# A two-layer kernel on one core: another order for tile 4, the transposes of tiles 1 and 5, and the bias rows of the feed-forward

## What is computed

```python
x = x + matmul(fake_quant(layernorm(x)), fake_quant(ctx_4096))      # ctx_4096 (2, 2048, 2048)
y = layernorm(x)
base_out = matmul(y, kernel) + bias                                  # kernel (2048, 2048), bias (2048,)
A_eff = einsum('bn,nri->bri', gate, lora_A)                          # y as 8 groups of 256 rows
B_eff = einsum('bn,nor->bor', gate, lora_B)
delta = B_eff (A_eff y) + lora_B_shared (lora_A_shared y)            # rank 32 each
out = x + base_out + delta
```

## Time and profile before

| | us |
|---|---|
| median of the runs | 1049.54 |
| profiled execution | 1046.42 |
| its span | 1044.9 |
| PE busy in it | 991.1 (95%), 4663 matmuls |
| DVE busy | 536.2 (51%) |
| ACT busy | 297.0 (28%) |
| POOL busy | 209.8 (20%) |
| share of PE in the chain that ended last | 71% |

### The profile page before, as it was taken

One profiled execution on the slowest core, in us unless ns is written; L12 is line 12 of the kernel. 1 busy time (PEld: TensorE's weight loads), 2 busy tenths in 40 slices (PEclk: granted clock), 3 DMA queues, 4 the chain that ended last, 5 costly groups with the idle time before them and its releaser, 6 DMA issues.

```text
span 1044.9 us, 12005 instructions
## 1 busy us (share of the span) xinstructions
PE 991.1 (95%) x4663; PEld 460.3 (44%) x4663; DVE 536.2 (51%) x756; ACT 297.0 (28%) x213; POOL 209.8 (20%) x233
## 2 busy tenths in 40 slices
PE   2898999898999999999999999998999999999996
PEld 1343444353544444444444444444554444444442
DVE  7766858968554565553423765877542032014010
ACT  4663422253131142232214521363230021012000
POOL 3001100021113013212411643320104004004010
PEclk9999999999999999999999999999999999999999
DMA  8699982859655346446699851767824024014010
GB/s 364 240 307 380 355 306 39 186 115 216 172 183 198 123 152 200 158 149 206 233 294 284 323 204 71 160 123 151 211 107 156 31 101 161 20 40 150 10 50 20
DMA packets 139863, 181.43 MB, mean 174 GB/s; under 512 B 112688, under 2 KB 112688, under 8 KB 127280
## 3 DMA queue, kind: packets, MB, share of 16 engines
q1 hardware_dynamic: 125040, 117.99, 39.1%
q0 software_dynamic: 13632, 58.73, 15.5%
q10 hardware_dynamic: 1152, 4.19, 1.0%
HBM read 124.26 MB, written 29.36 MB: 147 GB/s over the span
## 4 chain that ended last, share of the span: by engine, by line
PE 71%; DVE 10%; DMA 6%; ACT 5%; issue 4%; SPq 1%; POOL 1%; POOLq 0%; ACTq 0%; DVEq 0%
PE psum L1005 17%; PE psum L1187 16%; PE psum L1188 16%; PE psum L1189 16%; PE psum L1210 2%; DVE ring L1446 2%; DMA stage<-in_ctx_in 1%; PE psum L1067 1%; DVE hl L1492 1%; ACT ring L785 1%; DMA bias_sb<-in_bias 1%; DMA xn<-in_x 1%; DMA stage<-in_w 1%; PE psum L1199 1%; PE psum L1198 1%
## 5 line engine op out<-in xcount | busy, mean ns | idle before, releaser
L1187 PE MATMUL psum<-ring,lhs 128*128 128x512 f16 x1016 | 385.8, 380 | 12.6 <-issue 8.5
L1188 PE MATMUL psum<-ring,lhs 128*128 128x512 f16 x1016 | 385.8, 380 | 0.0
L1189 PE MATMUL psum<-ring,lhs 128*128 128x512 f16 x1016 | 385.6, 380 | 0.0
L1005 PE MATMUL psum<-ring,lhs 128*128 128x512 bf16 x1024 | 227.8, 381 | 3.6 <-DVE ring L1412 2.1
L1187 PEld LDWEIGHTS psum<-ring,lhs 128*128 128x128 f16 x1016 | 99.5, 98 | 135.2 <-issue 11.0
L1005 PEld LDWEIGHTS psum<-ring,lhs 128*128 128x128 bf16 x1024 | 100.3, 98 | 126.0 <-issue 4.2
L1189 PEld LDWEIGHTS psum<-ring,lhs 128*128 128x128 f16 x1016 | 99.6, 98 | 120.3 <-issue 0.8
L1188 PEld LDWEIGHTS psum<-ring,lhs 128*128 128x128 f16 x1016 | 99.5, 98 | 118.5 <-issue 0.5
L1499 DVE SCALAR_TENSOR_TENSOR x<-psum,sc,x 128x512 f32<-128x512 f32 (+1 forms) x64 | 45.2, 746 | 191.2 <-PE psum L1199 190.4
L649 POOL TENSOR_TENSOR x<-x,bias_sb 128x512 f32<-128x512 f32 (+1 forms) x64 | 86.6, 1377 | 190.9 <-ACT x L916 130.4
L785 ACT ACTIVATE ring<-stage,sc 128x2048 f16<-128x2048 f32 x32 | 63.6, 1999 | 170.1 <-PE psum L1189 137.8
(11 more groups left out here) (168 smaller groups left out, 656.5 us busy)
## 6 DMA issues: line engine op xcount, KB each, us to landing
stage<-in_w SPq DMA_DIRECT2D x38, 1024.0 KB, 6.3
stage<-in_ctx_in SPq DMA_DIRECT2D x30, 1024.0 KB, 8.1
out<-x POOLq DMA_DIRECT2D x64, 256.0 KB, 3.2
x<-in_x POOLq DMA_DIRECT2D x8, 1024.0 KB, 11.9
xn<-in_x POOLq DMA_DIRECT2D x8, 1024.0 KB, 6.8
x<-in_x POOLq DMA_DIRECT2D x4, 2048.0 KB, 14.7
lhs<-in_lora_a POOLq DMA_DIRECT2D x4, 1024.0 KB, 12.0
lhs<-in_lora_b SPq DMA_DIRECT2D x4, 1024.0 KB, 9.7
```

The source lines that it names most:

```text
L1005: last = pe.matmul(psum[:, t, :], lhs_q[:, k, t * P:(t + 1) * P], ring_q[:, g, j % 2, u, :], start=(k == 0), stop=(k == KT - 1 and not by_pe))
L1187: pe.matmul(psum[:, t, :], hi, ring[:, g, 0, u, :], start=(kk == 0), stop=False)
L1188: pe.matmul(psum[:, t, :], hi, ring[:, g, 1, u, :], start=False, stop=False)
L1189: last = pe.matmul(psum[:, t, :], lo, ring[:, g, 0, u, :], start=False, stop=False)
```

## The change

- SP: in block 0 both halves of tile 1 are transposed right behind tile 0, ahead of the load of weight group 2; before, the high half stood ahead of it and the low half behind it. Tile 5's transposes stand ahead of `load_a` 2.
- ACT: group 2 of block 0 is converted ahead of the root of tile 2. The split, the next root and the row term of tile 4 stand ahead of `product_p` 0 and `b_groups`.
- DVE: `product_p` 0 and the two `b_pair` stand behind tile 4 instead of behind tile 3.
- PE: in the pair, group 2's products with the top half of the weights (`top_group`) wait only for ACT's conversion; the products with the rest (`rest_group`) follow once DVE is done. The same matmuls in all.
- POOL: the bias row of block 0 is fetched by `first_bias` at the place of before; the rows of blocks 1 to 3 by `next_bias`, right after the sums of the block before (in batch 0's block 0 after the reduction of the maxima), so ahead of that block's stores and of the next loads of x.

```diff
@@ w_block @@
                         turn_y(b, 0)
-                        turn_high(b, 1)
-                    if g == 2 and isinstance(j, int) and j == 0:
-                        turn_low(b, 1)
+                        turn_y(b, 1)
@@ SP, block 0 @@
                 if b == 0:
                     w_peaks_block(1)
+                turn_y(b, 5)
                 load_a(b, 2)
-                turn_y(b, 5)
@@ POOL @@
             def add_bias(b, j, bb, reg):
+                pool.wait_ge(bias_in, (bb + 1) * 16)
                 if reg:
-                    pool.wait_ge(biased, bb * TILES)
                     pool.sem_inc(go, 1)
-                else:
-                    if b:
-                        pool.wait_ge(with_col, NBLK * TILES)
-                    pool.wait_ge(psum_full, (blk(b, 0, NBLK - 1) + 1) * TILES)
-                pool.dma_start(bias_sb[:, :], bias_row[:, bass.ds(j * NW, NW)].to_broadcast([P, NW])).then_inc(bias_in, 16)
-                pool.wait_ge(bias_in, (bb + 1) * 16)
                 for t in range(TILES):
...
+            def first_bias(b):
+                if b:
+                    pool.wait_ge(with_col, NBLK * TILES)
+                pool.wait_ge(psum_full, (blk(b, 0, NBLK - 1) + 1) * TILES)
+                pool.dma_start(bias_sb[:, :], bias_row[:, 0:NW].to_broadcast([P, NW])).then_inc(bias_in, 16)
+
+            def next_bias(j, bb):
+                pool.wait_ge(biased, (bb + 1) * TILES)
+                pool.sem_inc(go, 1)
+                pool.dma_start(bias_sb[:, :], bias_row[:, bass.ds(j * NW + NW, NW)].to_broadcast([P, NW])).then_inc(bias_in, 16)
...
+                first_bias(b)
                 add_bias(b, 0, blk2(b, 0), False)
                 if b == 0:
                     largest(4, MX_W, PW_W)
+                next_bias(0, blk2(b, 0))
                 store(b, 0, blk(b, 1, 0))
...
                     add_bias(b, j, j + blk2(b, 0), True)
+                    next_bias(j, j + blk2(b, 0))
                     if b + 1 < NBATCH:
                         for i in range(1, LNB):
@@ ACT, block 0 @@
                 split_hi(b, 1)
+                w_groups(b, 0, [2])
                 root(b, 1, 2)
-                w_groups(b, 0, [2, 3])
+                w_groups(b, 0, [3])
                 split_hi(b, 2)
...
                 norm2_rows(3)
+                norm2_rows(4)
                 product_p(b, 0)
                 b_groups(b, 0)
-                for t in (4, 5, 6):
-                    norm2_rows(t)
+                norm2_rows(5)
+                norm2_rows(6)
                 product_p(b, 1)
@@ PE @@
+            def top_group(t, g):
+                for u in range(GU):
+                    for h in range(2):
+                        y = lhs[:, h, g * GU + u, t * P:(t + 1) * P]
+                        pe.matmul(psum[:, t, :], y, ring[:, g, 0, u, :], start=False, stop=False)
+
+            def rest_group(t, g):
+                for u in range(GU):
+                    hi = lhs[:, 0, g * GU + u, t * P:(t + 1) * P]
+                    pe.matmul(psum[:, t, :], hi, ring[:, g, 1, u, :], start=False, stop=False)
...
-                    for g in range(2, NG):
-                        pe.wait_ge(converted, grp_w(b, 0, g) + 1)
-                        for t in range(2):
-                            base_group(t, g)
+                    pe.wait_ge(act_conv, act_w(b, 0, 2) + 1)
+                    for t in range(2):
+                        top_group(t, 2)
+                    pe.wait_ge(converted, grp_w(b, 0, 2) + 1)
+                    for t in range(2):
+                        rest_group(t, 2)
+                    pe.wait_ge(converted, grp_w(b, 0, 3) + 1)
+                    for t in range(2):
+                        base_group(t, 3)
@@ DVE, block 0 @@
                 for t in range(3, TILES):
-                    if t == 4:
+                    if t == 5:
                         product_p(b, 0)
                         for h in range(2):
                             b_pair(b, 0, h)
```

## The result

| | before | after |
|---|---|---|
| median of the runs, us | 1050.85 | 1044.13 (1041.86 to 1044.75) |
| ratio | | 0.9941, 95% interval 0.9925 to 0.9956 |
| profiled execution, us | 1046.42 | 1044.01 |
| its span, us | 1044.9 | 1042.4 |

The change takes 6 to 7 us off the median where 12.5 were forecast, and the time is 7 us above the forecast of 1037.0, just outside the range. Before and after stand within 2% of each other, as forecast. Note that the two profiled executions differ by only 2.4 us; the first experiment shows why. One timed execution of before, of 4784.78 us, and one of a later kernel, of 1621.07 us at a mean granted clock of 0.618, lie far outside the rest and enter no ratio.

The account below looks back on a forecast made before the run. PE's waits (15.8 us) and slow clock (1.7) bound what can be won. 0 - 0.2 + 2.15 + 3.44 + 2.96 + 1.7 - 0.3 + 2.7 = 12.5 us off the 1049.54 median gives 1037.0, range 1033 to 1043.

Parts of the forecast that it names:

- What bounds the kernel: PE, busy 95%; from 160 us only its 15.8 us of waits and 1.7 us of slow clock can be won.
- Tile 1: Transposes ahead of group 2's load: PE's 2.7 us given back later, 0 in batch 0, loss of 0.2 in batch 1.
- rival 3: Late group 2 delays tile 3, both batches; 8.4 us load costs 4 to 4.5; loss chance 0.07, slower than before 0.03.
- Tile 4: Done ahead of LoRA on VectorE, its transposes land before PE asks: waits of 2.15 and 3.44 us go.
- Tile 5: Transposes ahead of slab load_a(2) in batch 0: PE's 2.96 us gap goes, and 1.7 of slow clock behind it.
- rival 2: SP's queue in batch 0 spoils tile 5 (1 us) or last slab (2), slow stretch returns (1.7): 1041.4; chance 0.15.
- The last slab: load_a(3) in batch 0: PE arrives earlier than VectorE's chain gains, 0.3 us of new waiting, bounds 0 and 2.
- The bias row: Early fetch in batch 0's loop: second x load 6.7 us earlier, block 2's 2.7 us of waits gone, 4 spare.
- rival 1: Bias row is no cause: the load of x at 339.74 goes no earlier; 1039.7 us, chance 0.1.
- The range: 1033 to 1043 us around 1037.0, with group 2's landing and median drift below, three rivals above.
- The rule on the clock: An idle gap between PE's matmul bursts drops its clock; 1.7 us counted at tile 5, though a 3.44 gap showed none.

Follow-up runs that it names:

- the first experiment: The kernel before, run again with no edit: median 1050.85 us, profiled span 1050.6 us against 1044.9 in the profile the forecast used.
- the one-element operation: The changed kernel plus a one-element tensor_tensor on GpSimd behind each partition_all_reduce, to load its code back early: 1041.65 us, 0.9924 of before.

## Why the forecast was 7 us too low, point by point

Two terms of the sum failed: tile 1 (-0.2, and it cost 3) and the bias row (2.7, and it brought 0). The two terms of tiles 4 and 5 came, but not each from its own edit.

- **What bounds the kernel** was right: the gains and losses of all kernels are PE's waits and slow stretches. But the base was one execution with one slow stretch, and the second profile of the same kernel has five such lengths (17 us). The step "The median of the runs is 1049.54, 3.1 above it; off that it is 1037.0" carried the 3.1 us over as if no edit could touch them, though part of them is slow stretches. Of the 8.2 us between the spans of the second execution of before and of the change (1050.6 and 1042.4), 2.7 are waits (15.7 and 13.0) and some 6 are clock (7.6 us lost in slow stretches against 1.6).
- **Tile 1: "gives 0 in batch 0 ... a loss of 0.2" in batch 1.** It cost 3. In batch 0 the steps held in kind: load issued at 190.05 (189.3 forecast), ScalarE at 196.09 (195.5), short waits at groups 2 and 3, tile 3 0.5 late. The low half landed at 193.6, not 191.7, as 4.4 us is the landing of an undisturbed transpose and this one took 6.9. The step that failed is batch 1, where I wrote "the orders are the same and the waits smaller" and did not read the queue. There the load had gone out in time in which SyncE had nothing else to issue (668.54, the low half at 670.74); behind it, it lost not the length of an issue but the whole wait for y_lo(1), and then met three other transfers. This is near rival 3 in its mild form, 4 to 4.5 us for a load of 8.4 us: it took 5.9 in batch 0 and 8.9 in batch 1. I gave it 0.07. The landing time alone was not what I had to fear: the later issue cost more.
- **Tile 4: 2.15 + 3.44.** Right, step by step: high half at 227.16 (226.6 forecast), low half at 229.38 (228.6), landed at 234.0 (233.5), no wait in either batch. Its size was too small, because it also does what I put down to tile 5.
- **Tile 5: 2.96 + 1.7.** The gap and the stretch are gone, with the low half landing at 245.6 (245 forecast), but not by this edit. The step "load_a(2) ... held SP to 247.6 (7.78 us)" took the slab for the cause; the cause was the two weight loads in flight ahead of it. My rival 2 had it right ("whenever a transpose follows a 1 MB load"), and the term did not use it. Tile 4's part moves those 7 us earlier and the hold falls to 2.55. The edit is worth 1 to 2 us at a place that I had not looked at.
- **The last slab: -0.3.** It landed in time in batch 0. The wait that came instead is 0.66 us at 261.35 for VectorE's evict2: PE gained more than VectorE's chain, as I had written, but the first thing that PE needs from that chain is a free bank of PSUM and not the slab.
- **The bias row: 2.7.** 0. "The configuration starts at about 309.8: adds from 317.0" took 7.2 us for the reload, 12.7 were needed; with the slower adds that took 3.3 us of the 6.7. And "4 to spare" took the landing time of x as fixed at 5.7 us, when its issue moved right onto two weight loads, to 10.0. The outcome is that of rival 1 (1039.7, chance 0.1), for a reason that it did not name: x did go earlier. The laps even lost some: PE comes to blocks 2 and 3 earlier by what it won at tiles 4 and 5, and the chain that begins with x does not. There is a gap of 2.93 us where there were 1.24 and 1.47, with a slow stretch behind it, and one of 1.47 where there was none.
- **The range.** Rivals 1 and 3 came true together: 12.5 - 2.7 - 3.0 - 0.7 at evict2 is 6.1 us, what was measured. That it fits so well is in part luck, as it leaves out the 4.0 us that the laps lost and the clock's gain beyond 1.7. I had priced each rival by itself. The 1033 to 1043 took in each of the two and not both.
- **The rule on the clock** (the Trainium skill, TensorE: Matmul & The Clock Gate, "Why this matters for your kernels"): an idle gap between bursts drops the clock. The traces agree for 23 gaps of 31. The 3.44 us of the first profile, not followed by a slow stretch, had made me doubt it; the same gap in the second profile, 3.47 us, was.

Not settled: the parts don't add up exactly. 11.4 us for tile 4's part, 1 to 2 for tile 5's, 0 for the row and -3 for tile 1's make 9 to 10, and the change has 6.2; the change without tile 1's part has 9.1 with an interval of 3 us to both sides. Whether tile 4's part loses 2 us in company, or the intervals hide it, these runs don't tell. As half of its gain is clock, and a gap elsewhere can bring a slow stretch back, the parts need not add up. Nor was anything tried against the 2.6 us at tile 1's low half.

## What to carry to other kernels

When a step is moved past another on a queue that issues in order, ask what that queue did in the time between: a load that went out while the queue had nothing else is not late by an issue but by the whole wait of the step put ahead of it, and this has to be read in each batch by itself. A long issue of a transpose belongs to what is in flight ahead of it as much as to the transpose, so moving the transfers ahead of it may cure it alone. And a transfer that is issued earlier lands earlier only if it doesn't run into others there: when a chain starts from one load, let the loads that nobody waits for yet go behind it (4.5 us here for two waits).

## What the runs showed of the hardware

- **The clock.** The same program, much the same gaps: from 160 us on 3.4 us at 0.50 in one execution, 17 us in another. Of the gaps of 2.15 to 3.95 us 23 of 31 were followed by such a stretch; 3.44 and 3.45 us once each were not.
- **GpSimd's reload.** From MODIFY_POOL_CONFIG, or the end of the maximum, to the next operation: 6.7 us for the one-element operation at 283.80 and 7.2 in the kernel before, both with no transfer in flight; 9.3 with x and four stores beside it (and two weight loads in its last 2.6 us), 12.7 with x, two weight loads and four stores. The Trainium skill (GPSIMD Engine Reference, "Instruction dispatch") has one figure of about 6 us; the traces come near it in the quiet cases alone.
- **A DMA transpose behind 1 MB loads.** In block 0 its issue on SyncE takes 1.7 to 4.0 us when no load of weights is in flight (over 3.2 only right behind another transpose), 1.9 to 7.0 with one and 3.2 to 10.3 with two, slab or half tile. It lands behind them: the slab issued at 736.79 landed 12.3 us later, 1.7 us after the second load.
